# Routing one row tile later: logits, counts and places of a batch move back inside the next batch's projections

## The reference, cut to what matters

```
h = _L0_tok_ref(...)                      # image tokens from a state-space kernel, (8, 256, 256)
h = concatenate([h, txt], axis=1)         # (8, 768, 256)
h = h + attn(layernorm(h))                # 16 heads, 4 key/value heads
h = h + ffn(layernorm(h))                 # mixture of experts

# ffn, for every token row xf of the 8 * 768
logits = xf @ Wr + br                     # 8 experts
topk_w, topk_idx = top_k(logits, 2)
gate = one_hot(topk_idx) weighted with softmax(topk_w)
y_e = relu(xf @ W1[e] + b1[e]) @ W2[e] + b2[e]
out = sum_e gate_e * y_e
```

## Time and profile before

| what | value |
|---|---|
| median of 3 runs | 2252.08 us (2251.83 to 2252.51) |
| profiled execution, its own time | 2256.4 us |
| its span, first to last instruction | 2254.4 us |
| PE busy | 2051.4 us, 91% |
| DVE busy | 1771.6 us, 79% |
| ACT busy | 1071.3 us, 48% |
| POOL busy | 875.4 us, 39% |
| mean granted TensorE clock | 0.977 |

### The profile page before, as it was taken

The page is one execution under the profiler, slowest core; times in us unless marked ns, Lnnn a source line. Parts: engine busy times, 40 slices in busy tenths (PEclk is TensorE's granted clock), DMA queues, the critical chain, the costliest instruction groups (busy, mean ns, idle before and its releaser), DMA issues. The chain is left out here.

```text
span 2254.4 us, 59220 instructions
## 1 busy us (share of the span) xinstructions
PE 2051.4 (91%) x21098; PEld 1240.2 (55%) x21099; DVE 1771.6 (79%) x3227; ACT 1071.3 (48%) x2463; POOL 875.4 (39%) x831
## 2 busy tenths in 40 slices
PE   0469999999999999999999999988899959999998
PEld 0334444444444444444444444433688849999997
DVE  8889999999999999999999999998244443444443
ACT  2145556555655656556655665564111113444443
POOL 0026424444364344542642444230033443444443
PEclk9999999999999999999999999999998969999999
DMA  2145354443644544445435534543675638898985
GB/s 61 41 108 128 106 128 116 124 121 98 151 107 103 150 112 121 118 109 139 117 104 128 122 106 121 126 122 119 215 250 193 229 125 219 209 213 208 213 209 137
DMA packets 189542, 317.02 MB, mean 141 GB/s; under 512 B 48913, under 2 KB 127121, under 8 KB 189329
## 3 DMA queue, kind: packets, MB, share of 16 engines
q1 hardware_dynamic: 156640, 275.39, 45.0%
q0 software_dynamic: 19440, 25.58, 6.2%
q10 hardware_dynamic: 13248, 13.13, 1.7%
HBM read 214.75 MB, written 92.31 MB: 136 GB/s over the span
## 5 line engine op out<-in xcount | busy, mean ns | idle before, releaser
L767 ACT ACTIVATE a_prob<-ps_s,a_nmax 128x768 f32<-128x768 f32 x768 | 685.7, 897 | 577.2 <-DVE a_nmax L852 577.2
L852 DVE TENSOR_REDUCE a_nmax<-ps_s 128x1 f32<-128x768 f32 x768 | 694.3, 943 | 47.9 <-PE ps_s L693 42.7
L858 DVE STREAM_TRANSPOSE a_probT<-a_prob 128x768 f32<-128x768 f32 x768 | 700.4, 950 | 1.1 <-ACT a_prob L767 1.1
L693 PE MATMUL ps_s<-a_kT,a_qT 64*128 64x384 f32 x3072 | 612.3, 512 | 55.1 <-ACT a_prob L767 51.5
L700 PE MATMUL ps_o<-a_probT,a_vrep 32*64 32x384 f32 x12288 | 561.2, 491 | 6.5 <-DVE a_probT L858 5.0
L693 PEld LDWEIGHTS ps_s<-a_kT,a_qT 64*128 64x128 f32 x3072 | 258.8, 185 | 390.4 <-ACT a_prob L767 274.6
L829 POOL TENSOR_TENSOR a_o<-a_o,a_invrow 128x1536 f32<-128x1536 f32 x32 | 110.0, 3438 | 791.3 <-ACT a_o L775 791.3
L700 PEld LDWEIGHTS ps_o<-a_probT,a_vrep 32*64 32x64 f32 x12288 | 243.5, 132 | 293.5 <-issue 129.7
L498 POOL TENSOR_TENSOR a_prod<-a_raw,a_table 128x384 f32<-128x384 f32 x304 | 294.2, 1000 | 132.3 <-ACT a_raw L759 128.9
L1409 POOL DMA_INDIRECT out_dram<-e_y,e_row_i x103 | 160.5, 1558 | 231.9 <-DMA out_dram<-e_y,e_row_i 145.7
L1346 PE MATMUL ps_r<-e_xT,e_w 128*128 128x128 f32 x1648 | 202.0, 276 | 0.0
(11 more groups left out here) (221 smaller groups left out, 1301.2 us busy)
## 6 DMA issues: line engine op xcount, KB each, us to landing
e_w<-in_L_ffn_W_dram SPq DMA_DIRECT2D x103, 512.0 KB
a_qT<-q_d SPq DMA_DIRECT2D x124, 384.0 KB, 8.9
a_vrep<-v_d SPq DMA_DIRECT2D x128, 192.0 KB, 3.8
a_invrow<-inv_d SPq DMA_DIRECT2D x64, 384.0 KB, 5.2
oT_d<-a_o SPq DMA_DIRECT2D x32, 768.0 KB, 3.2
r_oT<-oT_d SPq DMA_DIRECT2D x64, 384.0 KB
q_d<-a_qp SPq DMA_DIRECT2D x31, 768.0 KB, 3.7
e_x<-xs_d SPq DMA_DIRECT2D x103, 132.0 KB
```

Source lines behind the costliest of these rows:

```text
L693: last = pe.matmul(S[:, s % 2, r, 0:HALF], qT[rows, par, 2 * hp + c, P * t:P * t + P], kT[rows, par, :], start=True, stop=True)
L767: act.activation(prob[:, s % RING, :].rearrange("p (r k) -> p r k", r=2), S[:, s % 2, :, 0:HALF], ACT.Exp, bias=nmax[:, s % RING:s % RING ...
L852: v.tensor_reduce(nmax[:, s % RING:s % RING + 1], S[:, s % 2, :, 0:HALF], AX.XY, ALU.max, negate=True).then_inc(max_ready, 1)
L858: v.transpose(turned(par, s), prob[:, s % RING, :]).then_inc(t_ready, 1)
```

## The change

Logits go from beside tile 2 to beside tile 3, and `choose` with them. Counts go from after tile 3 to after tile 4, and `place` with them. `turn` stays after tile 1. The threshold of the scatters is written with one less, so that each pair of scatters is held for the same addition as before.

```
@@ route
-    TURN_AT, LOGITS_AT, COUNTS_AT = 1, 2, 3
+    TURN_AT, LOGITS_AT, COUNTS_AT = 1, 3, 4
@@ route, scatter
                 if not (isinstance(b, int) and b == NB - 1):
-                    paced = (b + 1) * TT + COUNTS_AT + 4 + t
+                    paced = (b + 1) * TT + COUNTS_AT + 3 + t
                     hold(pool, h1_ready, min(paced, NB * TT + 3) if isinstance(b, int) else paced)
```

## The result

The changed kernel is slower: 2269.0 us against 2251.2 us (medians of 20 runs each), ratio 1.0057 with a 95% interval of 1.0037 to 1.0077. The ratio compares means and leaves out the four slowest runs of the changed kernel, those over 2283 us, so it is smaller than that of the two medians, 1.0079. The times also spread more here, from 2250 to 2291 us, where those of the kernel before lie between 2243 and 2263. The forecast was 2231.

The account below looks back on a forecast made before the run. PE, busy 91% of the span, was taken as the bound, losing time to waits and lower clock. Removing 7.95 us of waits and 15.3 of clock loss, about 23.1, was set at 21 for the median: 2252.1 - 21 = 2231, range 2225 to 2238.

Parts of the forecast that it names:

- the wait before the logits: Routing, batches 2 to 6: PE waits for ACT's copies, released by late increments; removing it gains 7.95 us.
- stretches at 1.2 GHz: Batches 3 to 5: PE at the lower clock, likely triggered by the wait; the whole 15.3 us taken as removed.
- The 23.1 us: Routing windows between turns: wait and clock loss together, as the plain difference from five windows of 25.39 us.
- `place` ahead of norm: End of a batch: norm begins 0.0 to 0.1 us later, covered by 1.35 us before the turn.
- the r_oT loads have room: SP's loads for the next batch: DMA share should reach 0.87 at 25.4 us a batch, busy but not full.
- rival B: Thin logits, not the wait, cause the clock dips; only 7.95 us go, giving 2244 us; chance 0.10.
- the one on the scatters: GpSimd's scatters: `idx_ready` comes about 3.5 us later, first three pairs run into the next batch, at no cost.
- a coincidence of scatters with SP's issues: At the turn: PE's increments come late, by about 2.35 us, where scatters and SP's issues run at once.
- the scatters' later end in `drain`: Batch 6's scatter ends about 3.5 us later, before batch 7's places are known: no cost.
- Rival A: Before the logits: increments held until PE pauses, so the 1.7 us wait moves along; 2252 us, chance 0.14.
- Rival C: Before the turn: `place` delays norm, PE waits in six batches; slower, 2266 us, chance 0.14.
- The 4.3 us between profile and median: Whole kernel: possibly a clock dip only in the profiled execution; median gain then 18.8 instead of 23.1, 21 taken.

Follow-up runs that it names:

- e9: Kernel before, its twelve scatters per batch let go in three groups of four, logits still beside tile 2: 2235.4 us, ratio 0.9932.
- e10: Changed kernel, its twelve scatters per batch let go in three groups of four: 2238.3 us, ratio 0.9946 to the kernel before.
- e1: Changed kernel run again unaltered, for a second profile and second set of times: 2275.7 us, ratio 1.0098 to the kernel before.
- e11: Changed kernel run a third time unaltered, for another profile: 2268.8 us, ratio 1.0097 to the kernel before.
- first profile: Profiled execution of the changed kernel in its original measurement, the fastest of the 20 runs: 2250.0 us, span 2248.1.
- e6: Kernel before with SP's weight loads issued only when tile 3 is projected, scatters as before: 2260.0 us, ratio 1.0.
- e5: Kernel before with the scatters of row tiles 3 and 4 held, like tile 5's, for a later addition, making two runs of six: 2248.9 us, ratio 0.9964.
- e8: Kernel before with both the scatters of row tiles 3 and 4 and SP's weight loads moved later: 2260.2 us, ratio 1.0019.
- e7: Changed kernel with its scatters in two groups, of four and of eight: 2255.1 us, ratio 1.0002 to the kernel before.

## Why the prediction was wrong

Right: the wait before the logits is ACT's late start on late increments of PE; it goes when the copies are in time; stretches at 1.2 GHz begin at it, and nearly all of them go with it. The 23.1 us that I read for both together are there in the windows of that profile: e9 saves 24.3 us in them. In the median less is gained: e9 is 15.7 us under the kernel before, and e10, the changed order with its increments on time at the turns, 12.8, where 18.8 to 23.1 were forecast. The profile that I read was 5.2 us above the median of its kernel's 20 runs, so reading one profiled execution is likely to have over-priced the gain; in e10 a further 3.4 us lie in `drain`, and the rest was not followed. Right too that `place` ahead of norm costs nothing between the turns (e10), that the r_oT loads have room (DMA share 0.82 to 0.85 at 25.16 us a batch in e9), and that the logits' thin matmuls run at full clock when nothing waits (rival B falls: e9).

The step that failed is the one on the scatters. I took the copies' lateness of 2.98 us as fixed and set 3.5 us against it, and I costed the later `idx_ready` at nothing, since nobody waits for the scatters' data. I named all that was needed: GpSimd's issues stood beside each late increment, and the first three pairs would now run over the turn. But I had tied the lateness to a coincidence of scatters with SP's issues, at hand in both kernels, and did not ask what a longer run of scatters does to it. The paragraph that shifted the scatters should have been carried into the one on the increments: in batches 3 to 6, six in a row with the turn behind them gave 2.8 to 3.0 us from turn to first copy and 3.8 to 4.0 to the third, eight or ten in a row with the turn inside gave 4.3 to 8.0 and 6.7 to 9.3 us (e1, e11 and the first profile). The same step put the scatters' later end in `drain` at no cost; it costs 3.4 us there, by the logits' increment.

Rival A named the outcome, the wait moving along, with the wrong cause: PE's pause lets nothing go (e1: 2.3 us more after it). Its price was therefore wrong as well. The wait is not the same 1.7 us but mostly anything from 0.7 to 3.5, and it can cost the clock in four batches instead of three. Rival C, the slower case, had the wrong place: no wait before the turns of batches 1 to 7 appeared in any profile of the changed kernel. The 4.3 us between profile and median, which I split, lie within the spread of the kernel before, whose 20 runs reach from 2243 to 2263.

The size of the loss is accounted for in kind, not to the microsecond. Profiles at 2250, 2266 and 2276 us differ by the number of batches in which the clock fell behind a wait (one, two, four), and their routing windows sum to 189.1, 201.2 and 214.1 us.

The Trainium skill (Perfetto Trace Analysis, section Tensor Engine Instruction) lets TensorE push its update when PSUM has acknowledged the bytes. In e9 and e10 the trace agrees in all batches from 1 to 6, 0.63 to 0.72 us from turn to copy. At the turns of the other kernels with a long run of scatters before or over them, it mostly does not: up to 8.0 us.

## What to carry to other kernels

A lateness read from one profile is not a constant: before it is spent against a new distance, ask what makes it, and whether the edit moves or lengthens that too. Here a queue that nobody waited for, GpSimd's scatters, set when another engine's semaphores arrived; letting them go in short groups was worth more than the reordering of the work that waited. Where runs of one kernel spread over nearly 2%, one profile can show a gain that the median does not have: take a second profile near the median before explaining.

## What the runs showed of the hardware that was not expected

Increments of PE can come late while GpSimd issues indirect DMAs in a long unbroken run: 128 rows each, 0.96 us to issue, 1.26 us apart. In batches 2 to 7 they were late at every turn over which a run of six or more lay that had begun 5.4 us or more before it: the first copy came 1.8 to 8.0 us after the turn instead of 0.63, and some increments arrived only up to 2.4 us after the run's last scatter. Behind a run of six that had ended 1.6 to 1.8 us before the turn the first copy came 2.8 to 3.4 us after it in eight batches of the kernel before and e6 and 1.5 us after it in one. It came on time in five: batch 7 of the kernel before and of e6, and batch 5 of e6 and batch 2 of e5 and e8, where no further scatter was issued before it. Groups of four with pauses of 2.0 us and more held nothing at the turns of e9 and e10; in e7, where such a group ended just at the turn, they cost up to 0.8 us.

Two things do not fit a rule of run length alone: the increments of the turn in `drain`, on time 8.4 us into a run of twelve, and in the same run the increment of the logits, 3.5 us late in the changed kernel. VectorE's increments were held too, by up to 1.0 us in e7. ACT's showed no delay where I looked: in batch 4 of the kernel before the logits began 0.05 us after the third copy had ended. Why increments are held is open: no run measured the scatters' descriptors or queue by themselves. The r_oT loads are not needed (batch 7 of e5, and `drain`, have none); whether they make it longer is open.

The granted clock fell from 2.4 to 1.2 GHz in or behind waits of PE of 1.7 to 3.5 us in most cases, and behind shorter ones of 1.3 us (first profile after, batch 5) and 1.0 us (e5, batch 3). It does not always fall: batch 6 of the kernel before waited as long as batches 3 to 5 and kept its clock, and batch 7 of e11 kept it with a wait of 2.2 us. By window times missing clock, a fall cost 3.4 to 7.2 us in the windows shown.
